# One causal mask product behind two score products instead of one behind each, in a fused attention and expert block

## The reference, cut to what matters

```python
x = L0_attn_x                                   # 1 x 2048 x 128, float32
h = _layernorm(x, axis=-1) * (1 + ca) + sa
q = _rotary((h @ Wq + bq).reshape(b, s, 16, 64))
k = _rotary((h @ Wk + bk).reshape(b, s, 4, 64))
logits = jnp.einsum('bqhgd,bkhd->bhgqk', qg, k) * scale      # four query heads to a key head
logits = jnp.where(jnp.tril(jnp.ones((s, s), bool)), logits, jnp.float32(-1e+30))
w = jax.nn.softmax(logits, axis=-1)
x = x + ga * (jnp.einsum('bhgqk,bkhd->bqhgd', w, v).reshape(b, s, 1024) @ Wo + bo)
x = x + gb * moe(_layernorm(x, axis=-1) * (1 + cb) + sb)
```

## Time and profile before

| | |
|---|---|
| median of 3 runs | 1238.19 us (1237.99 to 1241.21) |
| the profiled execution's own time | 1241.08 us |
| its span, from the first to the last instruction | 1238.9 us |
| lies around the span | 2.2 us |
| attention | about 29 to 1031 us of the span |
| mask products | 256 at line 1162 and 256 at line 1192 |

### The profile page before, as it was taken

How to read it: one execution, slowest core, us unless ns; L and a number is a source line. 1 busy time by engine, 2 the same in 40 slices (tenths; PEclk the granted TensorE clock), 3 DMA queues, 4 the chain that set the end, 5 groups by cost and what they waited for, 6 DMA issues and landing times.

```text
span 1238.9 us, 16497 instructions
## 1 busy us (share of the span) xinstructions
PE 1088.2 (88%) x5698; PEld 657.5 (53%) x5698; DVE 854.7 (69%) x1680; ACT 540.0 (44%) x1149; POOL 603.7 (49%) x649
## 2 busy tenths in 40 slices
PE   3589999999999999999999999999999973039993
PEld 2355555554565655455655554555565533029993
DVE  3647878777778786868787867778786658305553
ACT  2344544544445445454454545454544433014441
POOL 2733645645346565346446735445545233734441
PEclk9689999999999999999999999999999996559997
DMA  8000000000000000000000000000000006121104
GB/s 233 1 1 1 1 2 1 1 1 1 1 1 1 1 1 1 1 1 2 1 1 1 1 1 1 1 1 1 1 1 1 1 1 203 46 60 51 48 23 117
DMA packets 31921, 25.08 MB, mean 20 GB/s; under 512 B 8432, under 2 KB 26992, under 8 KB 31840
## 3 DMA queue, kind: packets, MB, share of 16 engines
q1 hardware_dynamic: 22272, 16.94, 4.6%
q0 software_dynamic: 2272, 4.72, 1.1%
q10 hardware_dynamic: 7296, 2.36, 0.8%
HBM read 15.62 MB, written 8.40 MB: 19 GB/s over the span
## 4 chain that ended last, share of the span: by engine, by line
PE 74%; DVE 12%; POOL 5%; issue 3%; DMA 2%; ACT 2%; ACTq 1%; SPq 0%; POOLq 0%; DVEq 0%
PE PS L1205 19%; PE PS L1159 12%; PE PS L1187 11%; PE PS L1189 9%; PE PS L1270 4%; POOL sent L614 3%; PE PS L1135 3%; PE PS L1224 3%; PE PS L1289 2%; DVE part_max L885 2%; PE PS L1172 2%; PE PS L1142 2%; PE PS L1215 2%; DVE full L901 2%; PE PS L1162 1%
## 5 line engine op out<-in xcount | busy, mean ns | idle before, releaser
L885 DVE TENSOR_REDUCE part_max<-PS 128x1 f32<-128x512 f32 (+2 forms) x576 | 340.3, 618 | 134.0 <-PE PS L1159 111.8
L692 ACT ACTIVATE full<-PS 128x512 f32<-128x512 f32 x384 | 223.5, 599 | 198.2 <-PE PS L1189 186.1
L1187 PE MATMUL PS<-rounded 128*128 128x512 f32 (+3 forms) x640 | 271.9, 425 | 5.9 <-ACT diag L701 2.4
L1159 PE MATMUL PS<-rounded 128*128 128x512 f32 (+3 forms) x640 | 250.1, 417 | 2.4 <-DVE V L866 1.3
L561 POOL TENSOR_TENSOR full<-full 128x512 f32<-128x512 f32 x128 | 164.4, 1315 | 155.5 <-PE PS L1205 154.5
L1189 PE MATMUL PS<-rounded 128*128 128x512 f32 (+3 forms) x640 | 233.5, 365 | 0.0
L701 ACT ACTIVATE diag<-PS 128x512 f32<-128x512 f32 (+3 forms) x256 | 111.4, 441 | 216.3 <-PE PS L1192 186.3
L589 POOL TENSOR_TENSOR rot_cos<-qkv_sb,cos_sb 128x320 f32<-128x320 f32 x64 | 60.3, 942 | 276.3 <-DVE qkv_sb L863 274.0
L1159 PEld LDWEIGHTS PS<-rounded 128*128 128x128 f32 x640 | 119.8, 193 | 139.0 <-DVE part_max L885 62.2
L1205 PE MATMUL PS<-full,V 128*64 128x512 f32 x768 | 190.0, 605 | 0.0
L1187 PEld LDWEIGHTS PS<-rounded 128*128 128x128 f32 x640 | 122.9, 192 | 80.8 <-ACT diag L701 27.0
(11 more groups left out here) (153 smaller groups left out, 1481.9 us busy)
## 6 DMA issues: line engine op xcount, KB each, us to landing
full<-in_L_ffn_experts_w_dram SPq DMA_DIRECT2D x16, 256.0 KB, 6.9
sent<-full SPq DMA_DIRECT2D x1, 2574.0 KB, 18.9
full<-sent SPq DMA_DIRECT2D x9, 264.0 KB, 2.9
full<-made SPq DMA_DIRECT2D x8, 256.0 KB, 5.1
out_dram<-XA SPq DMA_DIRECT2D x4, 256.0 KB, 2.8
made<-attnT,back_to POOLq DMA_INDIRECT x39, 2.2
wqkv<-in_L_attn_Wq_dram ACTq DMA_DIRECT2D x1, 512.0 KB, 4.4
bqkv<-in_L_attn_bq_dram ACTq DMA_DIRECT2D x1, 512.0 KB, 9.8
```

The lines of the kernel that those rows point to most:

```text
L692: nc.scalar.activation(full[:, k % QUADS, r, :], PS[:, bank, :], ACT.Exp).then_inc(probs_ready, 1)
L885: nc.vector.reduce_max(part_max[:, t, b:b + 1], PS[:, bank, 0:width], AX.X).then_inc(ring_dve, 1)
L1159: last = nc.tensor.matmul(PS[:, bank, 0:w], QT[:, ch % 2, h, t * P:(t + 1) * P], KT[:, 0, keys:keys + w], start=True, stop=not last_bank)
L1187: nc.tensor.matmul(o, KT[:, 0, keys:keys + P], QT[:, ch % 2, h, q0:BANK], start=True, stop=False)
```

## The change

Mask products no longer stand directly behind their product. In the diagonal chunk of the scores, both heads' products are made first and then both masks, as a step "mask" of its own; ScalarE's exponentials of these rows move to that step. In the maxima, the diagonal products of query tiles t and t + 1 (t = 0 or 2) are made one behind the other, then both masks ("diagmax"); the products b < ch of both tiles come ahead of them. Nothing is computed otherwise, and the number of products is the same. The placing of one list, the maxima of J = 4, starts later: at 2.97 instead of 2.82, and it ends at 3.9 instead of 3.88.

```diff
     def maxima(J, m):
-        return [("max", J, m, t, b) for t in range(TB) for b in range(J % N_J // PAIRS + 1)] + [("maxed", J, m)]
+        order = []
+        for t in range(0, TB, 2):
+            order += [("max", J, m, t + k, b) for k in range(2) for b in range(J % N_J // PAIRS)]
+            order.append(("diagmax", J, m, t))
+        return order + [("maxed", J, m)]
...
                 main += [("s", J, q, r, 0), ("s", J, q, r, 1)]
+                if q == J // PAIRS:
+                    main += [("mask", J, r, m) for m in range(2)]
...
-        place(max_steps(3), 2.01, 2.95), place(max_steps(4), 2.82, 3.88), place(max_steps(5), 4.02, 4.88),
+        place(max_steps(3), 2.01, 2.95), place(max_steps(4), 2.97, 3.9), place(max_steps(5), 4.02, 4.88),
...
-                    elif x[0] == "s":
+                    elif x[0] == "s" and x[2] < local(x[1]):
                         exps(x)
+                    elif x[0] == "mask":
+                        exps(("s", x[1], local(x[1])) + x[2:])
...
+                elif kind == "diagmax":
+                    for k in range(2):
+                        step(("max",) + x[1:3] + (x[3] + k, x[1] % N_J // PAIRS))
...
+                    if kind == "diagmax":
+                        for (t, _), bank in zip(blocks, banks):
+                            nc.tensor.matmul(PS[:, bank, t * P:(t + 1) * P], ident16[:], causal16[:, 0, :],
+                                             start=False, stop=True).then_inc(ring_filled, 1)
...
-                    if q == ch:
-                        last = nc.tensor.matmul(PS[:, bank, q0:q0 + P], ident16[:], causal16[:, 1, :],
-                                                start=False, stop=True)
-                    last.then_inc(scores_ready, 1)
+                    if q < ch:
+                        last.then_inc(scores_ready, 1)
+                elif kind == "mask":
+                    _, J, r, m = x
+                    bank = SCORES + n.at["s", J, local(J), r, m] % SCORE_BANKS
+                    nc.tensor.matmul(PS[:, bank, r * P:(r + 1) * P], ident16[:], causal16[:, 1, :],
+                                     start=False, stop=True).then_inc(scores_ready, 1)
```

More of the change, by code:

```diff
@@ L94, in weight @@
             return part * (3.78 if x[0] == "max" else 2.0)
+        if x[0] == "diagmax":
+            return 3.78 * (2 * x[3] + 3) / TB
         if x[0] == "gap":
@@ L97, in weight @@
         return {"pv": 2.1, "qmax": 1.5, "proj": 3.0, "low": 3.0, "qk": 3.5, "poolsum": 0.01, "maxed": 0.25,
-                "diagsum": 3.3, "quadsum": 0.01, "sum": 2.8, "rowsum": 12.6, "norm": 2.8, "modulation": 0.0,
+                "mask": 0.0, "diagsum": 3.3, "quadsum": 0.01, "sum": 2.8, "rowsum": 12.6, "norm": 2.8, "modulation": 0.0,
                 "out": 8.0}[x[0]]
     def maxima(J, m):
-        return [("max", J, m, t, b) for t in range(TB) for b in range(J % N_J // PAIRS + 1)] + [("maxed", J, m)]
+        order = []
[3 more added lines that the diff above has]
+        return order + [("maxed", J, m)]
     def max_steps(J):
@@ L232, in __init__ @@
                     "proj": [(x, "dve")], "qk": [(("q",) + x[1:], "act"), (("k",) + x[1:], "act")],
-                    "max": [(x, "dve")], "qmax": [(x, "act")], "rowsum": [(x, "dve")],
+                    "max": [(x, "dve")],
+                    "diagmax": [(("max",) + x[1:3] + (x[-1] + k, x[1] % N_J // PAIRS), "dve") for k in range(2)], "qmax": [(x, "act")], "rowsum": [(x, "dve")],
                     "out": [(x, "dve")],
@@ L1150, in step @@
                     last.then_inc(ring_filled, 1)
-                elif kind == "max":
-                    _, J, m, t, b = x
-                    taken(("k", J // PAIRS * TB + t))
+                elif kind in ("max", "diagmax"):
+                    J, m, t = x[1:4]
                     ch, h = J % N_J // PAIRS, 2 * (J % PAIRS) + m
[L1155 to L1162, removed]
-                                                start=False, stop=True)
-                    last.then_inc(ring_filled, 1)
+                    blocks = [(t, x[4])] if kind == "max" else [(t, ch), (t + 1, ch)]
+                    banks = []
+                    for t, b in blocks:
+                        taken(("k", J // PAIRS * TB + t))
+                        banks.append(ring_bank(("max", J, m, t, b)))
+                        w = (t + 1) * P if b == ch else BANK
+                        keys = key_at(J // N_J * TILES + b * TB)
+                        last = nc.tensor.matmul(PS[:, banks[-1], 0:w], QT[:, ch % 2, h, t * P:(t + 1) * P],
+                                                KT[:, 0, keys:keys + w], start=True, stop=b < ch)
+                        if b < ch:
+                            last.then_inc(ring_filled, 1)
+                    if kind == "diagmax":
+                        for (t, _), bank in zip(blocks, banks):
+                            nc.tensor.matmul(PS[:, bank, t * P:(t + 1) * P], ident16[:], causal16[:, 0, :],
+                                             start=False, stop=True).then_inc(ring_filled, 1)
                 elif kind == "qmax":
```

## The result

The changed kernel takes 1245.98 us (median; 1245.1 to 1246.89) against 1238.19 us: the ratio is 1.0046, 95% interval 1.0033 to 1.006. The ratio is an estimate over all runs and not the quotient of the two medians, which lie 7.8 us apart; the gains and losses in us that follow go by the ratios. The kernel is slower, by some 0.46% or 5.7 us, and its time lies outside the range that was forecast. The profiled execution's span went from 1238.9 to 1244.2 us.

What follows compares the result with a forecast made beforehand. TensorE bounds the attention, with VectorE as tight in some stretches. Saving 8.4 us, less 1.5 not arriving and 2.2 for the ring, plus 0.6 at group starts, gives -5.3: 1238.19 to 1233 us, range 1227 to 1243.

Steps and rivals of the forecast that it cites:

- The cost of a mask and of a pair: TensorE: a mask before wide fp32r products costs 0.12 us, a mask behind a mask 0.055.
- The scores' part: Scores' diagonal chunk on TensorE: about 0.06 us saved a pair, nothing for the narrowest row's pair.
- The exponentials: ScalarE's diagonal exponentials, starting later behind the masks, stay covered by the values, except in each group's first row.
- the 0.6 us of gain: Group starts: ring copies come ahead of the exponentials, gaining 0.6 us over three places, of 0 to 2.
- The ring and the twos: Diagonal pairs take two ring banks at once, VectorE gets the first 0.12 to 0.24 us later: 2.2 us lost, 4.4 at most.
- The placing of J = 4: That list of maxima does the same work in 0.93 instead of 1.06 of a J: counted at nothing, priced as a rival.
- VectorE and the ring take it back: slower: Rival: the denser J = 4 list runs late on VectorE, 8.8 us over four groups, giving 1242; chance 0.11.
- waits ahead of qmax: TensorE's waits for VectorE's last maximum, 7.7 us over 11 times: not to rise much; the VectorE rival's loss shows there.
- The masks in a row are no cheaper: Rival: distance between masks does not follow the clock; 1247 at 0.11 us, 1240 at 0.08; chance 0.09.
- the exponentials set the pace: Rival: 0.45 us lost at each of 128 pairs if the values don't cover; 25 such pairs give 1244; chance 0.04.
- The saving of the maxima's own masks: Maxima on TensorE: about 0.06 us saved a pair, nothing for tiles 0 and 1.

Runs made afterwards that it cites:

- x1_scores: Changed kernel with the old list of maxima and old J = 4 placing, so only the scores' masks stand in twos: 1233.66 us, ratio 0.996.
- z3_scores_first: x1_scores with both masks right behind the second head's products, and each group's first row with each mask behind its own product: 1234.28 us, ratio 0.9963.
- y2_own_masks: Changed kernel with scores' masks as before; maxima in the new list, each diagonal mask directly behind its product inside the pair: 1247.98 us, ratio 1.0064.
- y1_order: Changed kernel with scores' masks as before; maxima in the new order, but diagonals as steps of their own, each with its mask: 1247.15 us, ratio 1.0054.
- x3_place: Kernel before with nothing changed but the list of J = 4 placed at 2.97 to 3.9: 1239.72 us, ratio 1.0008.
- z1_after_282: Changed kernel with a second partial-maxima buffer and the list of J = 4 at 2.82 to 3.88 again: 1245.71 us, ratio 1.0053.
- z5_after_but_j4: Changed kernel with a second partial-maxima buffer and the list of J = 4 wholly as before (order, single masks, placing): 1248.0 us, ratio 1.0065.
- w3_maxima: Changed kernel with scores' masks as before, only maxima in twos, and the diagonal pair's placing weight raised (0.22 in the formula): 1238.48 us, ratio 0.999.
- z4_after_weights: Changed kernel with the diagonal pair's weight in the placing raised by VectorE's mean durations (0.22 in the formula): 1236.66 us, ratio 0.9977.
- w5_best: z4_after_weights with scores' masks right behind the second head's products and single masks in each group's first row: 1235.98 us, ratio 0.9973.
- w1_before: Kernel before with the placing weight of each single diagonal maximum raised (0.22 in the formula): 1238.47 us, ratio 0.999.

## Why the prediction was wrong, point by point

**The cost of a mask and of a pair: right.** A mask between wide fp32r products cost 0.12 us and a pair costs 0.18, as forecast. From the first mask to the second are 0.066 us in the median of the 256 such steps of the attention behind 72 us (0.055 to 0.07 but for a few), at the granted clock of 1.00, where 0.055 was taken; over 264 pairs this is 2.9 us less saving. By the Trainium skill's 81 ns a product ("TensorE: Matmul & The Clock Gate", section "Back-to-back issue gap") the estimate for a pair would have been 0.20 (0.08 and 0.12): the second mask adds 0.06 (0.18 less 0.12). The measurement decides against it here.

**The scores' part: right.** Three of four rows of each J save 0.06 us, over 32 J 5.8 us before what values behind a mask take off; measured alone, 4.9 us.

**The exponentials: covered, as said** (x1_scores has new waits for them at the starts of three groups only), but at a group's start the 0.6 us of gain did not come. The new wait is 1.17 us, not 0.85, and it and the old one for copies are worth the same (z3_scores_first).

**What failed is the step "The ring and the twos", together with "The placing of J = 4".** The prediction put the ring's price at 2.2 us, 4.4 at most, and gave the cause as VectorE getting the first bank 0.12 to 0.24 us late. The maxima's half lost 10 us, and not, in the main, for that cause: with own masks it still lost some 8 us (y2_own_masks), and as single steps most of it (y1_order). The placing was priced at nothing, for J = 4 alone, and there it was harmless (x3_place, z1_after_282, z5_after_but_j4). What it missed is that *every* list of maxima was placed anew, by a weight in proportion to columns, and that the pairs then stood too close ahead of handovers that TensorE waits for: more room behind them, by one number, took all of the maxima's loss away (w3_maxima). I had read VectorE's stretches by their busy share and not by what stands next in its queue.

**The rival "VectorE and the ring take it back: slower"** had the right engine, the right sign and nearly the right time, 1242, at a chance of 0.11. That was luck in part: it priced the list of J = 4 alone, with waits ahead of qmax, and those fell (7.7 to 5.6 us), while the list's placing by itself cost nothing that can be told. "The masks in a row are no cheaper" and "the exponentials set the pace" fell.

**The saving of the maxima's own masks** was counted at 0.06 us for each of 64 pairs, 3.8 us. Even with the raised weight the maxima in twos give nothing that can be told from before (w3_maxima), and with the scores' twos they do no better than the scores alone (z4_after_weights 0.9977 and x1_scores 0.996; w5_best 0.9973 and z3_scores_first 0.9963; the intervals of each two overlap). The fourth J is where the most is lost between z4 and x1: 26.29 against 25.50 us, 0.8 a group, with the ring wait of 1.2 us in it that is 4.9 us in the list above. The wait at that place comes with the placing of J = 4: in z5_after_but_j4 it is down to 0.8 us in all and the fourth J is as before, but the third is 1.4 longer than before. So taking away one wait there brings the next; an order that is free of both was not tried.

Open is why 0.22 is enough at the third J and 0.11 is not. Whether the raise would also mend the order with single steps (y1_order, whose loss stands at the projections) was not tried. A list that follows VectorE's time was not tried for the sums and projections, which have weights of their own.

## What to carry to other kernels

Where one list sets the order on every engine, a change that merges or reorders steps for one engine is a new schedule for all: price what stands directly ahead of each handover in the *other* engine's queue, not only that engine's busy share. If steps get a weight by which they are spread, try how the time answers to it when the order changes: here a weight by columns, harmless with single maxima (w1_before), cost 9 to 11 us with pairs, VectorE's own time from start to start brought back part of that, and a weight above it the rest. Read such time from start to start, not from durations. A wait's size in a list is no price either: x3_place has 4.7 us of waits at the projections that before lacks, and its time is that of before. And test each half of a change by itself: here one gained 4.9 us and the other lost 10.

## What the runs showed of the hardware

A VectorE maximum over PSUM has a fixed part: its record is 283 ns long for 128 columns, with 130 ns (413 - 283) to 139 ns (552 - 413) for each 128 more, so some 150 ns are there at any width. Back to back less than half of that is paid: from one start to the next are 0.20 us for 128 columns and 0.60 to 0.61 for 512, which leaves some 0.07 us besides the columns.

A bf16 mask behind another costs 0.06 us at the granted clock of 1.00, while a single one between fp32r products costs 0.12. The difference fits the distance of fp32r products of 128 columns, of which one follows another by 0.11 to 0.12 us (308.46 to 308.57 in the changed kernel) and whose weight loads nothing covers; no run took the load apart from the product.
